# A DCN ranker on one core: sixteen fields gathered row by row on SyncE and ScalarE instead of eleven, the end row in PSUM, and a new order on TensorE

## The reference

```python
x0 = emb[ids].reshape(B, -1)                 # ids (2048, 26), many beyond H: the last row is meant
x = x0
for i in range(3):
    s = x @ cross_w[i]
    x = x0 * s[:, None] + cross_b[i] + x
h = relu(x0 @ w1 + b1)
h = relu(h @ w2 + b2)
h = relu(h @ w3 + b3)
return sigmoid(concatenate([x, h], axis=1) @ out_w + out_b)
```

## Time and profile before

| what | value |
|---|---|
| median of 3 runs | 549.64 us |
| the profiled execution: its time, its span | 547.23 us, 545.4 us |
| TensorE matmuls: busy | 478.0 us, 88% of the span |
| VectorE, ScalarE, GpSimd: busy | 182.8, 103.8, 391.6 us |
| mean granted TensorE clock | 0.987 of full speed |
| chain that ended last: TensorE, GpSimd, DMA, VectorE, issue | 57%, 14%, 11%, 9%, 8% |
| row DMAs: SyncE, ScalarE; gathers: GpSimd | 896, 512; 405 |

### The profile page before, as it was taken

One profiled execution on the slowest core, in us unless ns is written; L12 is line 12 of the kernel. 1 busy time (PEld: TensorE's weight loads), 2 busy tenths in 40 slices (PEclk: granted clock), 3 DMA queues, 4 the chain that ended last, 5 costly groups with the idle time before them and its releaser, 6 DMA issues.

```text
span 545.4 us, 10919 instructions
## 1 busy us (share of the span) xinstructions
PE 478.0 (88%) x2876; PEld 438.4 (80%) x2876; DVE 182.8 (34%) x380; ACT 103.8 (19%) x187; POOL 391.6 (72%) x412
## 2 busy tenths in 40 slices
PE   0079599999989989997999989999899989999997
PEld 0069499998978879896888979788798968888896
DVE  5464623232242323223332312323232233323324
ACT  6486511011011111101111101111111011111111
POOL 5777567777777777777777777777777777777730
PEclk9999899999999999999999989999999999999999
DMA  7992111111111111111111111111111111111100
GB/s 231 223 360 74 22 25 28 26 29 28 27 28 26 30 26 29 29 28 29 27 27 30 28 29 29 26 28 28 26 28 29 30 25 29 28 26 28 27 14 2
DMA packets 20608, 25.15 MB, mean 46 GB/s; under 512 B 10135, under 2 KB 11122, under 8 KB 20546
## 3 DMA queue, kind: packets, MB, share of 16 engines
q0 software_dynamic: 12960, 13.30, 13.6%
q1 hardware_dynamic: 6288, 10.94, 5.9%
q10 hardware_dynamic: 1298, 0.21, 0.2%
HBM read 24.41 MB, written 0.01 MB: 45 GB/s over the span
## 4 chain that ended last, share of the span: by engine, by line
PE 57%; POOL 14%; DMA 11%; DVE 9%; issue 8%; ACT 2%; POOLq 0%; DVEq 0%; ACTq 0%
PE l_bank L700 45%; POOL x_raw L334 14%; DMA x_raw<-in_L_rec_emb,idx 10%; PE h_bank L700 5%; PE x_bank L714 4%; DVE x_raw L510 4%; DVE h L529 3%; PE l_bank L774 1%; ACT w_hi L352 1%; PE h_bank L785 1%; ACT h_bank L362 1%; DVE w_lo L495 1%; DMA ids<-in_r_ids 0%; PE h_bank L740 0%; DVE h1T_lo L522 0%
## 5 line engine op out<-in xcount | busy, mean ns | idle before, releaser
L334 POOL DMA_INDIRECT x_raw<-in_L_rec_emb,idx x405 | 390.7, 965 | 131.1 <-issue 108.8
L700 PE MATMUL l_bank<-w_hi,xT_hi 128*128 128x342 f32 (+1 forms) x624 | 144.8, 333 | 8.2 <-DVE xT_lo L517 8.2
L700 PE MATMUL l_bank<-w_lo,xT_hi 128*128 128x342 f32 (+1 forms) x624 | 139.0, 323 | 0.0
L700 PE MATMUL l_bank<-w_hi,xT_lo 128*128 128x342 f32 (+1 forms) x624 | 138.7, 323 | 0.0
L700 PEld LDWEIGHTS l_bank<-w_hi,xT_hi 128*128 128x128 f32 x624 | 105.4, 193 | 10.9 <-issue 5.0
L700 PEld LDWEIGHTS l_bank<-w_lo,xT_hi 128*128 128x128 f32 x624 | 108.1, 193 | 0.0
L700 PEld LDWEIGHTS l_bank<-w_hi,xT_lo 128*128 128x128 f32 x624 | 107.2, 191 | 0.0
L510 DVE COPY_PREDICATED x_raw<-past,end_row 128x256 f32<-128x256 int32 (+3 forms) x65 | 40.5, 624 | 164.2 <-DMA x_raw<-in_L_rec_emb,idx 164.0
L398 ACT ACTIVATE xT_hi<-x_bank 128x512 fp32r<-128x512 f32 (+3 forms) x66 | 33.5, 507 | 270.5 <-PE x_bank L714 263.3
L714 PE MATMUL x_bank<-identity,x_raw 128*128 128x128 f32 x208 | 35.0, 280 | 46.3 <-DVE x_raw L510 28.8
L714 PEld LDWEIGHTS x_bank<-identity,x_raw 128*128 128x128 f32 x208 | 23.9, 142 | 58.2 <-issue 57.6
(11 more groups left out here) (83 smaller groups left out, 280.8 us busy)
## 6 DMA issues: line engine op xcount, KB each, us to landing
ids<-in_L_rec_emb SPq DMA_DIRECT2D x896, 0.2 KB
w_raw<-in_L_rec_w SPq DMA_DIRECT2D x18, 512.0 KB, 22.2
ids<-in_L_rec_emb ACTq DMA_DIRECT2D x512, 0.2 KB
x_raw<-in_L_rec_emb,idx POOLq DMA_INDIRECT x405, 2.5
b_rows<-in_L_rec_b SPq DMA_DIRECT2D x1, 512.0 KB, 7.5
b_rows<-in_L_rec_b SPq DMA_DIRECT2D x1, 256.0 KB, 5.7
ids<-in_r_ids SPq DMA_DIRECT2D x1, 208.0 KB, 2.6
b_rows<-in_L_rec_b SPq DMA_DIRECT2D x1, 128.0 KB, 6.7
```

The lines of the kernel that those rows point to most:

```text
L334: pool.indirect_dma_start(out=dst, out_offset=None, in_=emb, in_offset=rows).then_inc(landed, 16)
L700: done = pe.matmul(bank[:, 0:b - a], x[:, k, :], w[:, k, a:b], start=(k == 0 and n == 0), stop=(k == last_k and n == 2))
```

## The change

- **Fields.** SyncE fetches field 24 in nine tiles (2, 4, 6, 8, 9, 10, 12, 14, 15), ScalarE field 25 in seven (3, 5, 7, 9, 11, 13, 15). GpSimd's gathers become 400; tiles 0 and 1 have 26, tiles 9 and 15 have 24, the others 25. SyncE now reads byte addresses from `at_bytes` as ScalarE does, 32 registers at a time; `sp_idx` is gone. ScalarE issues 64 rows a step, in shares of 8, 12, 4, 16, 12 and 12, and loads each share's registers on its own.
- **End row.** It is copied once into the last 64 columns of `x_bank[1]`, and `make_whole` reads it there.
- **Groups** become 4, 3, 4, 2; in the last tile chunks 0-3, 4-6, 7-8, 12, 9-10, 11, so that chunk 12 (fields 24 and 25, which no gather brings in tile 15) comes ahead of the last gathers.
- **Order.** In TensorE's step, half of layer 2 runs ahead of the first transposes; each later group is transposed two chunks ahead of its first use (`ahead`; one in tiles 14 and 15); layer 3 of tile t-1 moves behind the transposes of h1 of tile t, into `x_bank[0]`. VectorE merges group 0 of a tile at the start of its own step, and group 1 behind `h2_lo`. GpSimd's wait for layer 3 moves from field 6 to field 16.
- **End.** Layer 2 of tile 15 does the whole first half, then the second, with the first transposes of h2 in its middle; h2 comes in parts of 2, 1 and 1 chunks; the logits of the first 15 tiles are done early, and the last tile's sum is the bias of its sigmoid.

```diff
-    SIZES = [4, 4, 3, 2]
+    SIZES = [4, 3, 4, 2]
...
+    LAST_GROUPS = [[0, 1, 2, 3], [4, 5, 6], [7, 8], [12], [9, 10], [11]]
...
-    SP_TILES = [3, 5, 7, 9, 11, 13, 15]
+    SP_TILES = [2, 4, 6, 8, 9, 10, 12, 14, 15]
+    SP_REGS = 32
...
-    ACT_TILES = [4, 7, 10, 13]
+    ACT_TILES = [3, 5, 7, 9, 11, 13, 15]
-    ACT_REGS = 16
-    ACT_SHARES = [12, 4, 8, 8, 12]
+    ACT_SHARES = [8, 12, 4, 16, 12, 12]
...
+        end_bank = x_bank[1][:, 512 - E:512]
-        l3_bank = h_bank[1]
+        l3_bank = [x_bank[0]] * (TILES - 1) + [h_bank[1]]
...
-                for p in range(0, P, len(regs)):
-                    sync.load(regs, sp_idx[i:i + 1, p:p + len(regs)])
+                for p in range(0, P, SP_REGS):
+                    regs = [sync.alloc_register(f"sp_row{i}_{p + j}") for j in range(SP_REGS)]
+                    sync.load(regs, at_bytes[at_row[t]:at_row[t] + 1, p:p + SP_REGS])
                     for j, reg in enumerate(regs):
-                        row = sync.snap(reg, min_val=0, max_val=H - 1)
-                        sync.dma_start(sp_rows[i % SP_BUFS][p + j:p + j + 1, :],
-                                       emb[bass.DynSlice(row, 1), :]).then_inc(sp_landed[i % SP_BUFS], 16)
+                        at = sync.snap(reg, donate=True, min_val=0, max_val=(H - 1) * ROW)
+                        sync.dma_start(sp_rows[i % SP_BUFS][p + j:p + j + 1, :].bitcast(U8),
+                                       emb_bytes[:, bass.DynSlice(at, ROW)]).then_inc(sp_landed[i % SP_BUFS], 16)
...
-                if f == 6 and t > 2:
-                    pool.wait_ge(l3_done, t - 1)
                 if f == 16:
                     pool.wait_ge(h1_transposed, 2 * t)
+                    pool.wait_ge(l3_done, t - 1)
                     pool.wait_ge(x_transposed, NG * t + 1)
...
             def step(t):
+                fetch(ACT_SHARES[0])
                 x_hi(t, 0)
-                fetch(ACT_SHARES[0])
-                x_hi(t, 1)
                 fetch(ACT_SHARES[1])
                 h2_hi(t - 1)
                 fetch(ACT_SHARES[2])
+                x_hi(t, 1)
+                fetch(ACT_SHARES[3])
                 x_hi(t, 2)
...
-                fetch(ACT_SHARES[3])
+                fetch(ACT_SHARES[4])
                 x_hi(t, 3)
-                fetch(ACT_SHARES[4])
+                fetch(ACT_SHARES[5])
                 h1_hi(t)
...
-                                    end_row[:, :].rearrange("p (o e) -> p o e", o=1).broadcast_to([P, n, E])).then_inc(x_whole, 1)
+                                    end_bank.rearrange("p (o e) -> p o e", o=1).broadcast_to([P, n, E])).then_inc(x_whole, 1)
...
             def begin(t):
+                make_whole(t, 0)
                 x_lo(t, 0)
+                l2_out(t - 1)
+                h2_lo(t - 1)
                 make_whole(t, 1)
-                l2_out(t - 1)
                 x_lo(t, 1)
-                make_whole(t, 2)
-                h2_lo(t - 1)
-                x_lo(t, 2)
...
                 l1_out(t)
                 dots_out(t)
-                make_whole(t + 1, 0)
                 h1_lo(t)
+                l3_out(t - 1)
...
             def begin(t):
+                l2(t - 1, range(0, HB))
                 transpose_x(t, 0)
-                l2(t - 1, range(0, HB))
+                l2(t - 1, range(HB, K2))
                 l1(t, 0, slice(0, 1))
-                l2(t - 1, range(HB, K2))
+                transpose_h2(t - 1)
+                l1(t, 0, slice(1, -ahead(t)))
                 transpose_x(t, 1)
-                l1(t, 0, slice(1, 3))
-                transpose_h2(t - 1)
-                l1(t, 0, LAST)
-                l1(t, 1, slice(0, 1))
-                transpose_x(t, 2)
-                l3(t - 1)
-                l1(t, 1, slice(1, None))
+                l1(t, 0, slice(-ahead(t), None))
 
             def step(t):
                 begin(t)
+                for g in range(1, NG):
+                    l1(t, g, slice(0, -ahead(t)))
+                    if g < NG - 1:
+                        transpose_x(t, g + 1)
+                    l1(t, g, slice(-ahead(t), None))
+                transpose_h1(t)
+                l3(t - 1)
...
+                l2_last(t, 0, range(0, K2))
+                l2_last(t, 1, range(0, K2 // 2))
+                transpose_h2_last(t, 0)
+                l2_last(t, 1, range(K2 // 2, K2))
+                l3(t, H2_PARTS[0][:1])
+                transpose_h2_last(t, 1)
+                transpose_h2_last(t, 2)
+                l3(t, H2_PARTS[0][1:])
+                l3(t, H2_PARTS[1], 1)
+                l3(t, H2_PARTS[2], 2)
...
-            act.activation(result[:, :], logits[:, :], ACT.Sigmoid).then_inc(result_ready, 1)
+            act.activation(result[:, 0:TILES - 1], logits[:, 0:TILES - 1], ACT.Sigmoid).then_inc(result_ready, 1)
+            act.wait_ge(h3_read, TILES)
+            act.activation(result[:, TILES - 1:TILES], h3_dots[:, TILES - 1:TILES], ACT.Sigmoid,
+                           bias=term[:, TILES - 1:TILES]).then_inc(result_ready, 1)
```

More of the change, by code:

```diff
@@ L30, in dcn_ranker_kernel @@
     assert sum(SIZES) == K1
-    LAST_SIZES = [4, 3, 2, 2, 1, 1]
-    LAST_GROUPS = [list(range(sum(LAST_SIZES[:g]), sum(LAST_SIZES[:g + 1]))) for g in range(len(LAST_SIZES))]
-    assert sum(LAST_SIZES) == K1
+    LAST_GROUPS = [[0, 1, 2, 3], [4, 5, 6], [7, 8], [12], [9, 10], [11]]
+    assert sorted(sum(LAST_GROUPS, [])) == list(range(K1))
     def groups(t):
@@ L274, in _ @@
             sync.wait_ge(sp_idx_ready, 1)
-            regs = [sync.alloc_register(f"sp_row{j}") for j in range(8)]
             for i, t in enumerate(SP_TILES):
@@ L453, in last_step @@
                 x_hi(t, 0)
+                h2_hi(t - 1)
                 x_hi(t, 1)
-                h2_hi(t - 1)
                 x_hi(t, 2)
-                x_hi(t, 3)
                 if t in SP_TILES:
                     sp_place(t)
-                for g in range(4, len(LAST_GROUPS)):
+                if t in ACT_TILES:
+                    act_place(t)
+                for g in range(3, len(LAST_GROUPS)):
                     x_hi(t, g)
@@ L502, in make_whole @@
                 if t == TILES - 1:
-                    dve.wait_ge(gathered_last[g], 16 * sum(of_pool(t, f) for f in range(a, a + n)))
+                    if any(of_pool(t, f) for f in range(a, a + n)):
+                        dve.wait_ge(gathered_last[g], 16 * sum(of_pool(t, f) for f in range(a, a + n)))
                 else:
@@ L601, in cross_logits @@
                 link(dve.tensor_scalar(term[:, :], scale[:, :], consts[:, CROSS - 1:CROSS], out_b_rows[:, 0:1], ALU.add, ALU.add))
+                dve.wait_ge(h3_read, TILES - 1)
+                dve.tensor_tensor(logits[:, 0:TILES - 1], term[:, 0:TILES - 1], h3_dots[:, 0:TILES - 1],
+                                  ALU.add).then_inc(logits_ready, 1)
             def first_step():
@@ L644, in last_step @@
                 l3_out(t - 1)
-                for g in range(3, len(LAST_GROUPS)):
+                for g in range(2, len(LAST_GROUPS)):
                     make_whole(t, g)
@@ L690, in _ @@
             last_step(TILES - 1)
-            dve.wait_ge(h3_read, TILES)
-            dve.tensor_tensor(logits[:, :], term[:, :], h3_dots[:, :], ALU.add).then_inc(logits_ready, 1)
         @block.tensor
@@ L717, in l1 @@
             def l1(t, g, part=slice(None), first=False):
-                ks = groups(t)[g][part]
+                ks, last = groups(t)[g][part], groups(t)[-1][-1]
+                if not ks:
+                    return
                 if ks[0] == 0 and t > 0:
@@ L743, in transpose_h1 @@
             def transpose_h1(t):
+                if t > 0:
+                    pe.wait_ge(h2T_ready, t)
                 for half in range(2):
-                    if half == 1 and t > 0:
-                        pe.wait_ge(h3_ready, t)
                     h1_chunks(t, h_bank[half], range(half * HB, (half + 1) * HB))
@@ L786, in transpose_h2, with transpose_h2_last, l3 @@
                 done.then_inc(h2_transposed, 1)
-            def transpose_h2_last(t):
-                for half, bank in enumerate(H2_LAST):
-                    pe.wait_ge(h2_ready, t + half + 1)
-                    for i in range(K3 // 2):
-                        k = half * K3 // 2 + i
-                        done = pe.transpose(bank[:, i * P:(i + 1) * P], h2[:, k * P:(k + 1) * P], identity[:, :])
-                    done.then_inc(h2_transposed, 1)
-            def l3(t, halves=1):
+            def transpose_h2_last(t, i):
+                pe.wait_ge(h2_ready, t + i + 1)
+                for j, k in enumerate(H2_PARTS[i]):
+                    done = pe.transpose(H2_LAST[i][:, j * P:(j + 1) * P], h2[:, k * P:(k + 1) * P], identity[:, :])
+                done.then_inc(h2_transposed, 1)
+            def l3(t, ks=range(0, K3), part=0):
                 if t == 0:
@@ L799, in l3, with ahead @@
                     pe.wait_ge(hi_split, len(LOADS))
-                for half in range(halves):
```

(24 more changed lines are left out.)

144 lines of the change are left out of this document (79 added, 65 removed).

## The result

The changed kernel takes 537.08 us (median of 4 runs, 536.77 to 538.74); the kernel before, run beside it, 550.27 (4 runs, 549.58 to 551.36). The ratio is 0.9765, 95% interval 0.9736 to 0.9793: 13.2 us faster. Of the two profiled executions the one after takes 536.77 us (span 535.0), the one before 547.23 (span 545.4), a difference of 10.4 in span. The other 2.8 lie between the profiled executions and the medians; their cause stays partly open.

A forecast was written before the change was run, and what follows sets the result against it. GpSimd's gathers were taken as the bound to about 512 us, TensorE only in the last 20. The terms -5.0 - 6.9 + 4.6 + 0.0 - 0.1 - 0.9 - 0.2 = -8.5 took 549.64 to 541.1 us, range 534 to 549.

The forecast's parts named there:

- Fewer gathers: GpSimd ahead of tile 15: 4 gathers fewer (376 against 380) at 1.249 us each, -5.0 us.
- the end row: Merge reading the end row from PSUM: gathers no longer stretch beside it, -6.9 us (between 0 and 7.5).
- Rival 3: Gathers beside the merge: the stretches stay, giving 548 us; chance 0.12.
- The start: First tiles: GpSimd newly waits at tile 2's field 16, which goes at 99.3 us; +4.6 us (0 to +6).
- Rival 4: Start: nothing waits at tile 2's field 16, or TensorE gets through quicker, giving 536.5 us; chance 0.18.
- The last two tiles: Tile 15's start to its h1 transposes: 40.2 us against 40.3 before, -0.1 us.
- The end: Behind tile 15's layer 2: half of h2 done under it, -0.9 us; logits add off the path, -0.2 us.
- SyncE: SyncE's 1152 rows: 0.403 us each (0.393 to 0.417), last issued at 502.7, with 10 us to spare.
- ScalarE: ScalarE's 64 rows a step: 28.1 us of its sequencer in 31.2, about 1 us slack at each x_hi; middle tiles 0.
- x_hi over 1 us late in every tile: ScalarE's x_hi: starting late by over 1 us in every tile would show the prediction wrong.
- TensorE stall 2 to 3 us at the third group: TensorE at the third group: an expected sign was a stall of 2 to 3 us a tile.
- The level: Whole kernel: the median of the runs lies 2.4 us above the profiled execution, carried over to the forecast.

The follow-up runs named there:

- a_405: The changed kernel with SyncE's fields cut to tiles 4, 9, 12 and 15, so 405 gathers: 544.72 us, ratio 1.0006 to the kernel before.
- b_sizes_psum: The kernel before with groups of 4, 3, 4, 2 and the end row read from PSUM: 540.07 us, ratio 0.9934.
- a_end_sbuf: The changed kernel with the end row read from SBUF again: 541.85 us, ratio 0.9966 to the kernel before.
- a_again: The changed kernel, unchanged, run again in a later set: 539.33 us, ratio 0.9927 to the kernel before.
- b_again: The kernel before, unchanged, profiled again on chip 10: 549.05 us, ratio 0.9995 to itself.
- a_end_order: The changed kernel with the last layer 2's halves multiplied chunk by chunk side by side, all h2 transposes behind them: 539.45 us, ratio 0.9831 to the kernel before.
- a_sp8: The changed kernel with SyncE loading 8 registers at a time instead of 32: 569.29 us, ratio 1.0484 to the kernel before.
- a_no16: The changed kernel without GpSimd's three waits at field 16: 537.53 us, ratio 0.9885 to the kernel before.
- a_share: The changed kernel with ScalarE's shares 8, 12, 4, 12, 16, 12: 538.58 us, ratio 0.9918 to the kernel before.
- b_fields: The kernel before with the change's new fetching by SyncE and ScalarE alone, in the old order: 560.44 us, ratio 1.0287.
- a_ahead1: The changed kernel with each group transposed one chunk ahead in all tiles, not two: 543.02 us, ratio 0.9873 to the kernel before.

## Why the prediction was right, and where it was off

It gave 541.1 (534 to 549) and the result is 537.1: the sign, the chain of reasons and the range held, the sum was 4.0 us short. About 2 of that lie in the start, about 2 in the level, and both are things that differ from one execution to the next.

**Fewer gathers and the end row: right.** The prediction took -5.0 and -6.9 between the start and tile 15, together -11.9; from tile 2's field 16 to tile 15 the profiles give 385.1 - 397.2 = -12.1. Of the first term, 4 gathers at 1.25 are 5.0, and a_405 bears out the full price; the remaining 7.1 are the second, against 6.9. b_sizes_psum, with only the group sizes beside it, shows 7.5 for it. In the changed kernel the end row alone is worth 2.8 of them in the trace (a_end_sbuf) and 2.5 in time, for with the new order fewer gathers begin inside a merge; so part of the 7.1 would have come from the order alone. Rival 3 (the stretches stay) falls. The rule that the prediction quoted from the Trainium skill (SBUF — State Buffer, "Who interferes with whom") is borne out by 2 to 7 gathers over 1.0 us with PSUM against 17 to 41 without. Its other page (VectorE: DVE Perf Modes, the errata section) would have made the merge 0.065 us longer; the traces have 0.728 and 0.730 from PSUM (the change and a_again) against 0.739 and 0.738 from SBUF (before and a_end_sbuf). The measurement decides: for this operation the page's 62 cycles don't hold.

**The start: the right mechanism; the size was luck.** The term was +4.6, measured +2.6. The wait came where it was put, at tile 2's field 16, and was 3.2 us long against "some 3". But everything in front of it was 2 us earlier than forecast: h1's bias add of tile 0 begins at 53.68, where 54.89 was the time before and 0.4 more the forecast. Most of that is TensorE's clock, in two places. Behind the stall of 4.6 us at the end of the weight splits it had a mean of 0.61 over 62 to 68 us and 0.73 over 68 to 72 before, which the forecast carried over; in the change it was 0.72 and 1.00. And earlier TensorE stands still for about 2 us until a group's low part is there: before, ahead of the second group (2.11 us), in the change, with its smaller second group, ahead of the third (1.94). The 27 matmuls behind that stall, before, in the change and in a_again, which is the same kernel once more:

```profile
39.20 6.07 PE l_bank L700 x27
```
```profile
44.47 4.51 PE l_bank L714 x27
```
```profile
43.98 6.04 PE l_bank L714 x27
```

And the stretches that they lie in (us, busy and count by engine, then granted clock, DMA share, GB/s), in the same order:

```profile
39.00:44.00 5.00, 4.80 (x21) 4.80 (x22) 3.21 (x6) 4.91 (x8) 3.78 (x5) 0.66 0.76 248
```
```profile
44.00:50.00 6.00, 5.54 (x36) 5.52 (x37) 3.69 (x7) 4.08 (x7) 4.46 (x6) 1.00 0.14 29
```
```profile
44.00:50.00 6.00, 6.00 (x30) 5.98 (x30) 2.85 (x5) 3.22 (x5) 4.48 (x6) 0.72 0.19 36
```

The clock fell behind the stall in the profile before and not in that of the change, and in a_again it fell. The stall of 1.9 us ahead of the third group stands in all eleven profiles with the new group sizes (2.2 in a_405); over 44 to 50 us the clock stayed at 1.00 in four and fell to a mean of 0.72 in seven. The second profile of the kernel before (b_again, 1.35 us at 38.76) kept 1.00. What decides it isn't shown. So the smaller second group saved no time by itself, and one pair of profiles can't size this term: field 16 of tile 2 goes at 97.24, 98.28, 98.23, 98.76 and 98.86 in the five profiles whose start is the change's (after, a_again, a_end_order, a_sp8, a_end_sbuf), and at 94.67 and 92.54 in the two of before. On chip 10 the difference is 5.7 us (a_end_order less b_again). The forecast's 4.6 lies between. Rival 4's 536.5 is closer to the result, but its first mechanism, no wait at field 16, didn't happen; its second, TensorE quicker through the start, did in this execution. Without the wait (a_no16) field 16 goes 1.9 us earlier and the kernel gains 1.8.

**The last two tiles: -0.1, measured -0.5.** From tile 15's start to h1's transposes 39.64 us, before 40.13. I had let ScalarE's rows cost 0.9 in tile 14; they cost 0.5 there (layer 1 waits from 482.75 to 483.23).

**The end: -1.1, measured -0.5** (11.09 against 11.55). From the end of layer 2 to the sigmoid's it is 3.63 instead of 4.32, 0.7 of the 1.1 that I had there. I counted one transpose and one chunk of layer 3 behind layer 2; two single chunks of h2 come there, each with its transpose, its ScalarE and its VectorE step, and the last 6 matmuls begin only at 530.85. And I left out the piece in the middle: h2's transposes lengthen layer 2 by 0.23.

**SyncE: right.** A row takes 0.398 against 0.403 (bounds 0.393 and 0.417), load of 32 2.13 against 2.33, last row at 495.3 against 502.7. Chunk 12's merge in tile 15 begins at 512.56, some 14 us behind what 495.3 and 3 us for landing and placing ask for. a_sp8 bears it out: its last row is 48 us later, 14 of these are spare, and its span is 33 to 35 us longer than those of the two profiles of the change.

**ScalarE: partly wrong.** I gave it about 1 us of slack at each x_hi and put its cost at nothing in the middle tiles. In the early tiles the chain of waits runs through its rows (ACTq 12% of it), and x_hi of the third group comes behind 16 rows each time. One of the prediction's own signs of being wrong, x_hi over 1 us late in every tile, was nearly there: 1.0 to 2.4 us in 11 of 14 tiles. It would have been a false alarm, for GpSimd's 31.2 us a tile (25 gathers) cover TensorE's 28.6 and such waits as long as the clock stays full: a_share takes the waits away and gains 0.7, which isn't clear of noise; b_fields and a_ahead1 have waits of 2 us in each tile, the clock falls behind 9 and 5 of them, and they lose 16.7 and 4.5. Nor did TensorE stall 2 to 3 us at the third group: it stalls 1.1 to 1.4 at the second, behind h2_lo, in tiles 2 to 13, and 0 to 1.6 at the third.

**The level.** I carried over that the median lies 2.4 above the profiled execution; after the change it lies 0.3 above. Before, stretched gathers vary from run to run (8.4 us in one profile, 13.0 in another); now there are hardly any. That may make part of the difference. What it doesn't explain is chip 7, on which the kernel before takes 543.9 and the change gains 4.6 us instead of 13.2; the kernel before was not profiled there, so it stays open whether its gathers collide less on it. The parts taken singly there do fit the small gain: 5.4 for five gathers (a_405) and 2.5 for the end row (a_end_sbuf), less what the start costs.

## What to carry to other kernels

Where an engine issues at a fixed rate and its mean duration lies above its median, look at what runs beside the long ones: here 20 ns in the mean of 405 gathers were 7 us in the first comparison. When work is moved to the queues of other engines, ask what stands behind it in program order: the same 64 rows a tile cost next to nothing, 4.5 or 16.7 us (the last with the 5 us of the saved gathers already taken off), by which copy they stood ahead of and how early that was needed. And when a wait grows, look at the granted clock behind it before calling the wait covered: most of the 4.5 and the 16.7 was the clock. Last, don't size a term of 2 us in the start from one pair of profiles; two executions of the same kernel differed by that much.
